# Causal masks of a transformer megakernel: mask products on TensorE against a minimum on the probabilities, with another order of values, loads and row pieces

## The reference

```python
x = _layernorm(x + _L0_attn_ref(x, ...))          # causal self attention, 16 heads of 16
x = _layernorm(x + _L0_xattn_ref(x, ctx_768, ...)) # cross attention, 1024 keys
x = _layernorm(x + _L0_ffn_ref(x, ...))           # soft mixture, 8 experts
x = _layernorm(x + _L1_attn_ref(x, ...))          # causal self attention
x = _layernorm(x + _L1_xattn_ref(x, ctx_768, ...))
x = _layernorm(x + _L1_ffn_ref(x, ...))           # causal self attention, then top-2 of 8 experts
```

```python
scores = jnp.where(causal, scores, -jnp.inf)
weights = jax.nn.softmax(scores, axis=-1)
out = jnp.einsum('bhqk,bhkd->bhqd', weights, v)
```

## Time and profile before

| | |
|---|---|
| runs | 2868.8, 2875.1, 2877.04 us |
| profiled execution | 2872.66 us, span of the core 2870.9 us |
| mean granted TensorE clock | 0.945 |
| TensorE busy | 2526.0 us, 88% |
| VectorE busy | 1494.8 us, 52% |
| ScalarE busy | 1330.3 us, 46% |
| GpSimd busy | 444.9 us, 15% |

### The profile page before, as it was taken

How to read it: one execution, slowest core, us unless ns; L and a number is a source line. 1 busy time by engine, 2 the same in 40 slices (tenths; PEclk the granted TensorE clock), 3 DMA queues, 4 the chain that set the end, 5 groups by cost and what they waited for, 6 DMA issues and landing times. The chain is left out here.

```text
span 2870.9 us, 47221 instructions
## 1 busy us (share of the span) xinstructions
PE 2526.0 (88%) x15793; PEld 1449.9 (51%) x15794; DVE 1494.8 (52%) x4176; ACT 1330.3 (46%) x2833; POOL 444.9 (15%) x687
## 2 busy tenths in 40 slices
PE   6999999999869889997899999999987994499991
PEld 3555544444334456675456544444444553266661
DVE  2555877888544500023555788777745654222224
ACT  2655466667744412111455567666664551022220
POOL 4222221101100000000123212202122001400004
PEclk8999999999999999999899999999998995599996
DMA  7544534233000022114644533242132317311103
GB/s 222 160 134 137 141 85 103 52 78 78 1 1 0 1 95 93 62 48 141 178 131 127 144 93 93 60 107 85 47 94 83 97 51 249 128 33 33 33 29 94
DMA packets 153825, 259.89 MB, mean 91 GB/s; under 512 B 22713, under 2 KB 96705, under 8 KB 149441
## 3 DMA queue, kind: packets, MB, share of 16 engines
q1 hardware_dynamic: 150544, 248.81, 29.9%
q0 software_dynamic: 3072, 8.39, 0.9%
HBM read 180.71 MB, written 81.53 MB: 91 GB/s over the span
## 5 line engine op out<-in xcount | busy, mean ns | idle before, releaser
L1444 ACT ACTIVATE second_p<-psum 128x512 f32<-128x512 f32 (+3 forms) x1024 | 461.5, 522 | 250.4 <-PE psum L1286 246.9
L1444 ACT ACTIVATE first_p<-psum 128x512 f32<-128x512 f32 (+3 forms) x768 | 366.7, 548 | 180.0 <-PE psum L1286 177.2
L1536 DVE TENSOR_REDUCE second_max_parts<-psum 128x1 f32<-128x512 f32 x512 | 323.0, 684 | 72.5 <-PE psum L1263 70.7
L1536 DVE TENSOR_REDUCE first_max_parts<-psum 128x1 f32<-128x512 f32 x512 | 323.0, 684 | 62.6 <-PE psum L1263 61.2
L1532 DVE CUSTOM_DVE_ANT_0 second_masked<-psum,mask_qk 128x384 f32<-128x384 f32 (+3 forms) x512 | 229.3, 488 | 198.1 <-PE psum L1263 168.0
L1298 PE MATMUL psum<-second_p,second_v_aug 128*32 128x512 f32 (+3 forms) x2048 | 236.0, 533 | 8.7 <-ACT second_p L1444 8.3
L1263 PE MATMUL psum<-second_k,second_q 64*128 64x512 f32 (+3 forms) x1024 | 201.0, 390 | 40.1 <-DMA second_k<-a_k_parts 27.4
L1276 PE MATMUL psum<-second_q,second_k 64*128 64x512 f32 (+3 forms) x1024 | 224.1, 434 | 3.3 <-DVE second_max_parts L1536 1.0
L1286 PE MATMUL psum<-second_shift_T,choose 64*128 64x512 f32 (+3 forms) x1024 | 196.9, 380 | 0.0
L1298 PE MATMUL psum<-first_p,first_v_aug 128*32 128x512 f32 (+3 forms) x1536 | 185.6, 555 | 10.5 <-ACT first_p L1444 10.5
L1276 PEld LDWEIGHTS psum<-second_q,second_k 64*128 64x128 f32 x1024 | 97.4, 186 | 186.0 <-ACT second_p L1444 78.1
(11 more groups left out here) (337 smaller groups left out, 3759.2 us busy)
## 6 DMA issues: line engine op xcount, KB each, us to landing
first_k<-c_k_parts SPq DMA_DIRECT2D x64, 256.0 KB, 4.7
second_q<-a_q_parts SPq DMA_DIRECT2D x128, 128.0 KB, 2.9
second_k<-a_k_parts SPq DMA_DIRECT2D x128, 128.0 KB, 2.9
second_k<-c_k_parts SPq DMA_DIRECT2D x64, 256.0 KB, 4.8
first_q<-a_q_parts SPq DMA_DIRECT2D x64, 128.0 KB, 2.9
first_k<-a_k_parts SPq DMA_DIRECT2D x64, 128.0 KB, 2.9
c_k_parts<-first_held SPq DMA_DIRECT2D x16, 512.0 KB, 3.0
first_q<-c_q_parts SPq DMA_DIRECT2D x64, 128.0 KB, 4.4
```

What stands on the lines that cost most here:

```text
L1444: evacuated(act.activation(probs[tile % 2][:, 2 * h + p, q0:SEQ], bank[:, q0:SEQ], ACT.Exp, scale=scale), event)
L1536: evacuated(v.reduce_max(max_parts[n % 2][:, h, p, qt, k0 // BANK:k0 // BANK + 1], bank[:, 0:width], axis=AX_X), event)
```

## The change

The mask products of `scores` go, with their constants `pick` and `mask_kq` (eight VectorE casts at the start). In their place stands a constant `past_kq`, 3e38 where a query may see a key and 0 for future keys, and a new event `cut` on VectorE: once a tile's exponentials are done, the diagonal block of its probabilities (128 x 4 heads x 128) becomes the minimum of itself and `past_kq`. In causal layers the values product waits for the cut in place of the exponentials.

In the plan, a tile of a causal group is now: scores of pair 0; units; the cut of the tile before (in tile 1 then augment, load, vload, with the load first); scores of pair 1; units; the values product of the tile before (and the drain behind a group's last one); in tile 1 the turn; chain; pieces. In cross groups the values product stays between the two score pairs and only the turn moves behind the second pair and its units. In the last two groups of a stage, which have no units to hand out, cut and values come after the second pair. Of the pieces, the slot rows of group 20 get a second REST ahead of them. For a2's first three batches the scaled rows come with three RESTs and four front pieces, and five front pieces go to the next group. For its last batch the `apply` of c1 moves from the end of group 33 into group 34, the scaled rows get two RESTs and stay in group 35 with three front pieces, four go to group 36, and two to group 37 ahead of the output pieces there.

```diff
...
+            pool.memset(c.past_kq[:, :], MOST).then_inc(filled, 1)
...
+            pool.affine_select(out=c.past_kq[:, :], in_=c.past_kq[:, :], compare_op=ALU.is_ge, fill=0.0,
...
-            for dst, src in ((c.pick, c.ident_bf), (c.mask_kq, tri_kq)):
-                for own in (slice(0, 64), slice(64, P)):
-                    for x in range(2):
-                        v.tensor_copy(dst[own, x, :], src[64 * x:64 * x + 64, :]).then_inc(c.made, 1)
...
+    def cut(of):
+        if of and layer_of(of[0]).causal:
+            plan.append(("cut", *of))
+
+    def values(of):
+        if of:
+            plan.append(("values", *of))
+            if of[1] == layer_of(of[0]).key_tiles - 1:
+                plan.append(("drain", of[0], 0))
+
+    def further(n):
+        if n + 1 < groups:
+            plan.append(("augment", n + 1, 0))
+        if NB <= n + 3 < groups:
+            plan.append(("load", n + 3, 0))
+        if n + 3 < groups:
+            plan.append(("vload", n + 3, 0))
...
-            plan.extend([("values", n - 1, last), ("drain", n - 1, 0), ("turn", n - 1, 0)])
+            last = (n - 1, layer_of(n - 1).key_tiles - 1)
+            cut(last)
+            values(last)
+            plan.append(("turn", n - 1, 0))
...
+            before = (n, t - 1) if t else (n - 1, layer_of(n - 1).key_tiles - 1) if n else None
             plan.append(("scores", n, (t, 0)))
-            share(units, 2 * t + 1, 2 * steps)
-            if t:
-                plan.append(("values", n, t - 1))
-            elif n:
-                plan.extend([("values", n - 1, layer_of(n - 1).key_tiles - 1), ("drain", n - 1, 0)])
-            if t == 1:
-                if n:
-                    plan.append(("turn", n - 1, 0))
-                if n + 1 < groups:
-                    plan.append(("augment", n + 1, 0))
-                if n + 3 < groups:
-                    plan.append(("vload", n + 3, 0))
-                if NB <= n + 3 < groups:
-                    plan.append(("load", n + 3, 0))
+            if n + 2 < groups:
+                share(units, 2 * t + 1, 2 * steps)
+                cut(before)
+                if not layer.causal:
+                    values(before)
+                if t == 1:
+                    further(n)
             if t == steps - 1 and n + 1 < groups:
                 plan.append(("shift", n + 1, 0))
             plan.append(("scores", n, (t, 1)))
             share(units, 2 * t + 2, 2 * steps)
+            if n + 2 >= groups:
+                cut(before)
+            if n + 2 >= groups or layer.causal:
+                values(before)
+            if t == 1 and n:
+                plan.append(("turn", n - 1, 0))
+            if t == 1 and n + 2 >= groups:
+                further(n)
             if n + 1 < groups and t < 3:
...
-                    if layer.causal:
-                        for x in range(2):
-                            for h in range(2):
-                                own = slice(64 * h, 64 * h + 64)
-                                pe.matmul(bank_of(event, h)[:, q0:q0 + 64 * (x + 1)], c.pick[own, x, :],
-                                          c.mask_kq[own, x, 0:64 * (x + 1)], start=False, stop=False)
...
-                    wait_evacuated(pe, ("scores", n, (t, 1)), 1)
+                    if layer.causal:
+                        pe.wait_ge(cut, cut_at[n, t] + 1)
+                    else:
+                        wait_evacuated(pe, ("scores", n, (t, 1)), 1)
...
+                def cut_future(event):
+
+                    _, n, t = event
+                    for p in range(2):
+                        wait_evacuated(v, ("scores", n, (t, p)), 1)
+                    own = probs[value_at[n, t] % 2][:, :, t * P:(t + 1) * P]
+                    v.tensor_tensor(own, own, c.past_kq[:, :].unsqueeze(1).to_broadcast([P, GH, P]), ALU.min).then_inc(cut, 1)
...
-        pieces[GROUPS * BATCH + GROUPS] = [REST] + slot_pieces()
+        pieces[GROUPS * BATCH + GROUPS] = [REST, REST] + slot_pieces()
...
-                pieces[first + 2] = [REST, REST] + scaled_rows(slot) + whole[:5]
-                pieces[first + 3] = whole[5:]
+                pieces[first + 2] = [REST] * 3 + scaled_rows(slot) + whole[:4]
+                pieces[first + 3] = whole[4:]
             else:
-                pieces[first + 3] = scaled_rows(slot) + whole[:5]
-                pieces[first + 4] = whole[5:]
+                apply = pieces[first + 1].pop()
+                pieces[first + 2] = [REST, apply, REST, REST]
+                pieces[first + 3] = [REST, REST] + scaled_rows(slot) + whole[:3]
+                pieces[first + 4] = whole[3:7]
+                pieces[first + 5] = whole[7:] + pieces[first + 5]
```

More of the change, by code:

```diff
@@ L108, in stage_constants @@
     c.ident_bf = c.keep("ident_bf", [P, P], BF16)
-    c.pick = c.keep("pick", [P, 2, P], F32R)
     c.choose = c.keep("choose", [P, 2, P], F32R)
     c.mask_qk = c.keep("mask_qk", [P, SEQ])
-    c.mask_kq = c.keep("mask_kq", [P, 2, P], F32R)
+    c.past_kq = c.keep("past_kq", [P, P])
     c.eps = c.keep("eps", [P, 1])
@@ L116, in stage_constants @@
     filled = c.sem("const_filled")
-    with (nc.sbuf_tensor("tri_kq", [P, P], BF16) as tri_kq,
-          nc.sbuf_tensor("chosen", [P, 2, P], BF16) as chosen, nc.Block() as block):
+    with nc.sbuf_tensor("chosen", [P, 2, P], BF16) as chosen, nc.Block() as block:
         @block.sync
@@ L126, in _ @@
         def _(pool):
-            for t in (c.ident, c.ident_bf, c.mask_qk, tri_kq):
+            for t in (c.ident, c.ident_bf, c.mask_qk):
                 pool.memset(t[:, :], 0.0).then_inc(filled, 1)
+            pool.memset(c.past_kq[:, :], MOST).then_inc(filled, 1)
             pool.memset(chosen[:, :, :], 0.0).then_inc(filled, 1)
@@ L150, in _ @@
         def _(v):
-            v.wait_ge(c.made, 5)
-            for dst, src in ((c.pick, c.ident_bf), (c.mask_kq, tri_kq)):
-                for own in (slice(0, 64), slice(64, P)):
-                    for x in range(2):
-                        v.tensor_copy(dst[own, x, :], src[64 * x:64 * x + 64, :]).then_inc(c.made, 1)
             v.wait_ge(filled, 17)
@@ L158, in _ @@
             v.wait_ge(c.made, CONSTANTS)
-CONSTANTS = 5 + 8 + 1
+CONSTANTS = 5 + 1
 @staged
@@ L650 @@
 CREST = CTX_D - P
-LEAST = -3.0e38
+LEAST, MOST = -3.0e38, 3.0e38
 SLOT_LEAST, ROW_LEAST = 1e-24 / D, (1e-12 / 16) ** 2 * 1e-5
@@ L784, in body @@
         if n == groups:
-            last = layer_of(n - 1).key_tiles - 1
-            plan.extend([("values", n - 1, last), ("drain", n - 1, 0), ("turn", n - 1, 0)])
+            last = (n - 1, layer_of(n - 1).key_tiles - 1)
+            cut(last)
+            values(last)
+            plan.append(("turn", n - 1, 0))
             plan.extend(x for x, _ in own)
@@ L843, in stage_attentions @@
     ring_at = {"S": {}, "U": {}}
-    bank_at, users = {}, []
+    bank_at, users, cut_at = {}, [], {}
     for event in plan:
@@ L852, in stage_attentions @@
             value_at[n, x] = len(value_at)
+        elif kind == "cut":
+            cut_at[n, x] = len(cut_at)
         elif kind == "apply":
@@ L959, in stage_attentions @@
         stored = [sem(f"stored{i}") for i in range(HELD)]
-        augmented = sem("augmented")
+        augmented, cut = sem("augmented"), sem("probabilities_cut")
         chained, value_done = sem("chained"), sem("value_done")
@@ L1693, in _ @@
                         statistics(event)
+                    elif kind == "cut":
+                        cut_future(event)
                     elif kind == "aggregate":
```

1 line of the change is left out of this document (removed).

## The result

The changed kernel takes 2993.0 us (median of 4 runs, 2987.4 to 3000.4) against 2874.7 of the kernel before on the same chip: the ratio is 1.042, with a 95% interval of 1.038 to 1.045. The forecast was slower, 2946, with 2850 to 2990 as its range; the time lies 3 us outside it. The direction and the place were right, the size wasn't: +118 us against +72. The profiled execution took 3000.4 us (span 2998.6), 128 more than that of before.

A forecast was written before the change was run, and what follows sets the result against it. TensorE was taken to bound the kernel (88% busy), VectorE four self groups. Terms 81 + 20 + 8 + 4 - 13 - 4 - 12 - 9 - 3 = +72 on 2872.7, plus 2.4 for the median, gave 2946 us; range 2850 to 2990.

The forecast's parts named there:

- VectorE takes unit A before the cut: In self tiles the cut stands behind the first unit's row maxima on VectorE; values and TensorE's queue wait, 1.55-2.35 us.
- The cut at 0.69 us: Duration of each of 192 minima on VectorE, 0.69 us, or 0.74 with the semaphore; bounds 0.6 and 1.5.
- 4.4 us of wait per loaded group: TensorE's wait in self groups whose tiles carry project or output steps; less masks +2.9 us each, +81 over 28.
- Bare groups of 12.8: The 13 self groups carrying no units or pieces would take about 12.8 us against 11.3, +20 in all.
- The masks give back 1.45 us a group, 70 us: TensorE time regained from dropped mask products, eight score events a group, over 48 self groups; bounds 65 and 135.6.
- The other edits, -41: Reordering of values, loads, row scaling and turns outside the cut: -13, -4, -12, -9 and -3 us.
- The last batch: Loads before vload and a later apply end a 10.1 us TensorE idle in the row-scaling group: -12 us.
- the cross groups with row or slot turns: Row turns placed a tile behind the scaling wait less for VectorE in three batches: about -9 us, bounds -16 and 0.
- GpSimd and the cut, +14, left out of the sum: A quarter of 28 x 4 cuts meet GpSimd and lose half a microsecond: +14, some +30 by the skill's port rule.
- The clock falls as well, 12%, +34: Rival, 12%: waits in every tile cause some 20 half-clock stretches of TensorE, 1.7 us each: +34, 2980 us.
- How the numbers follow: Step turning cases into odds for the whole kernel: faster 16%, same 4%, slower 80%, range 2850 to 2990 us.
- Cut as reckoned: Main case, 68%: self groups wait as computed, 2946 us, own range 2905 to 2985, GpSimd in or out.

The follow-up runs named there:

- e4: Changed kernel with VectorE's cut of the tile before moved ahead of the tile's first unit: 2847.4 us, 0.992 of the kernel before.
- e8: Changed kernel with a self tile's values product moved behind the tile's own piece, the cut left in place: 2848.2 us, 0.992 of the kernel before.
- e7: Changed kernel without the cut, mask products back, values behind the first unit as in the kernel before; other edits stay: 2814.1 us, 0.980.
- e6: Changed kernel with GpSimd's subtraction behind a project piece shortened from 512 to 16 columns (part of the computation left out): 2943.3 us, 1.023.
- e5: Changed kernel where TensorE repeats the products of a self tile's second unit while it would wait for the cut: 2975.8 us, 1.035.
- e11: Changed kernel with both the repeated products in the wait and GpSimd's subtraction of 16 columns: 2954.2 us, 1.029.
- e9: Changed kernel with neither cut nor mask products, values behind the first unit as in the kernel before: 2762.5 us, 0.963.
- e1: Changed kernel without the cut and without mask products, values still behind the second unit: 2809.7 us, 0.979.
- e12: Changed kernel with the cut ahead of the first unit and values behind the tile's piece, but behind the first unit in VectorE-bound groups: 2805.9 us, 0.978.

## Why the prediction was wrong in size, by its own steps

- *VectorE takes unit A before the cut, and TensorE's queue stands behind the values*: right, and it is the cost (e4, e8).
- *The cut at 0.69 us*: right (median 686 ns) where GpSimd is quiet.
- *4.4 us of wait per loaded group*: right in sum in groups without a split piece (4.4), but by some luck, as 0.5 of it is the values' later place; too much in those with a split piece (3.5 without collisions). Bare groups of 12.8: 13.1.
- *The masks give back 1.45 us a group, 70 us*: right in loaded groups (1.25 to 1.5), too much in bare (0.8) and VectorE-bound ones (0.6 to 0.8 where the clock is the same); 51.6 us in all.
- *The other edits, -41*: -58.5 by e7 (-62.5 in its profiled execution, to which the following numbers belong). The last batch (-13.5) and the last cross groups (-10) came about as said, the cross groups with row or slot turns gave 13 instead of 9. A group is 0.17 us shorter with the later turn, which had been put at 0; over 80 groups that is up to 14 us, 11 of them outside the groups just named. The last two self groups gave 7 with masks; with the cut in them they gave nothing. Some 8 us are left for the load order, which had been put at 3.
- *GpSimd and the cut, +14, left out of the sum*: **this is the first step that failed.** Its price is 50 us (e6). The quarter of 28 x 4 cuts was right (29 beside the subtraction), the half microsecond wasn't (0.83 each), and what followed from it was missing: with the longer waits 61 us of half clock. The other side pays as well, where the cut comes first: the subtraction's maximum is 1781 ns, its median 1276. The Trainium skill (SBUF — State Buffer, the section on two separate sides) states that whichever of the two instructions starts first holds the shared pair of ports for its whole length. This trace agrees, in the 29 cases and in the 13. The forecast's estimate by that rule was +30, nearer to the 27 us of longer cuts than the +14, though not to the 50.
- *The clock falls as well, 12%, +34*: **the second**, as it was given 12% and left out of the sum. It fell: 190 us of half clock instead of 53, some 32 to 45 us of time by e5, e11 and the runs' own scatter (of which nearly half goes when the collisions go). The size of +34 is luck: it was to be 20 stretches of 3.4 us at 1.7 us each, and it was twice as many (137 us more) at 0.8 to 1.2 us each.
- *How the numbers follow*: **the third.** Cut as reckoned, collisions and clock were treated as cases that exclude each other, and the range was drawn from them one at a time. They add up, and each makes the other likelier: a longer wait is also a longer pause. 2946 + 14 + 34 is 2994, about what was measured, but term by term it isn't the same sum. The wait for the cut and all that hangs on it cost 230 us (changed kernel less e9) against 113 + 70 = 183 by the forecast: 50 for the collisions, some 20 for the rest of the clock (32 to 45 less the 15 to 21 in e6), and 160 for the wait itself and the later values, which by themselves are 47 (e1 less e9). So the wait was put too high, and by that the error is smaller than what was left out. The masks gave 52 instead of 70, the other edits 58 instead of 41. +47 + 18 - 17 = +48, and the result is 47 above the forecast. (The forecast's own terms give 2872.7 + 2.4 + 72 = 2947; the 2946 is a slip of 1 us.)

How the collisions' 50 us and the clock's 32 to 45 divide stays open; they overlap by some 15 to 21 us. Two versions weren't tried: masks in the VectorE-bound groups with the cut elsewhere, and masks with the values behind the piece as in e12. So e12 and e7 compare the best of four places for the cut with the better of two for the masks.

## What to carry over

When an in-order queue waits for a new step on another engine, the price is set by what that engine has queued ahead of the step: look for the place one line further up before judging the step itself (146 us here, with the collisions and the clock that went with the wait). Price a new two-input VectorE instruction beside each GpSimd instruction that runs in the same tile, with what the longer wait then does to TensorE's clock: such prices come together, and a forecast that chooses between them leaves one out. They don't add in full either: the short subtraction gave 50 us, the filler 17, both together 39. And an edit that seems to move a product only past another one (values behind unit B) can cost on a third engine, here 25 to 47 us.

## What the runs showed of the hardware

- With pauses ahead of the values (1.24 us in the tile shown) and TensorE at work in between, the clock was at 1.2 GHz for 190 us of 957; with the same pauses filled by repeated products for 57 of 933, and in the kernel before for 53 of 813. Two bare groups with the same work can differ, 1.00 and 0.73. The Trainium skill (TensorE: Matmul & The Clock Gate, the section on a second HAM failure mode) tells of another kernel in which small idle times between groups of products, there from cycling through PSUM banks, make the clock go back and forth between its two levels. This trace agrees, with pauses of another origin.
- A minimum over 128 x 4 x 128 fp32 with two inputs in SBUF takes 686 ns alone and up to 1726 when a GpSimd subtraction of 1276 began before it (29 cases). When the minimum began first (13 cases), it kept its 0.69 us and the subtraction took 1657 to 1781.
- A us at 1.2 GHz instead of 2.4 cost this kernel 0.24 to 0.34 us of time, by the estimate under e5.
